# Scores of two slots in one stretch, softmax one slot ahead, in an attention and FFN kernel

## The reference

```python
def attention(query, key, value, mask, w_q, w_k, w_v, w_o):
    q = (query @ w_q).reshape(b, sq, 16, 64).transpose(0, 2, 1, 3)
    k = (key @ w_k).reshape(b, sk, 16, 64).transpose(0, 2, 1, 3)
    v = (value @ w_v).reshape(b, sk, 16, 64).transpose(0, 2, 1, 3)
    scores = einsum('bhqd,bhkd->bhqk', q, k) / sqrt(64)
    scores = where(mask, -inf, scores)
    out = einsum('bhqk,bhkd->bhqd', softmax(scores), v)
    return out.transpose(0, 2, 1, 3).reshape(b, sq, 1024) @ w_o

x = x + attention(layernorm(x), ctx, ctx, mask, w_q, w_k, w_v, w_o)
n = layernorm(x)
x = x + n @ int4_grid(kernel) + bias + (n @ lora_a) @ lora_b
```

## Time and profile before

| | |
|---|---|
| median of 3 runs | 492.87 us (491.85 to 492.99) |
| the profiled execution | 492.92 us, of which span 491.0 us |
| granted TensorE clock, mean | 0.987 |
| TensorE matmuls busy | 448.6 us, 91% of the span |
| VectorE busy | 405.4 us, 83% |
| GpSimd busy | 389.4 us, 79% |
| ScalarE busy | 329.7 us, 67% |
| DMA | 70.34 MB, mean 143 GB/s |

### The profile page before, as it was taken

One profiled execution on the slowest core, in us unless ns is written; L12 is line 12 of the kernel. 1 busy time (PEld: TensorE's weight loads), 2 busy tenths in 40 slices (PEclk: granted clock), 3 DMA queues, 4 the chain that ended last, 5 costly groups with the idle time before them and its releaser, 6 DMA issues.

```text
span 491.0 us, 15523 instructions
## 1 busy us (share of the span) xinstructions
PE 448.6 (91%) x5879; PEld 326.3 (66%) x5879; DVE 405.4 (83%) x1116; ACT 329.7 (67%) x851; POOL 389.4 (79%) x647
## 2 busy tenths in 40 slices
PE   3879989899999999999999999999999999989984
PEld 1435646786667866777666866777766866677772
DVE  4886689897988889787997979888988988888872
ACT  5968656866568766776677766776677766676631
POOL 5786777999788978789788988888787978688821
PEclk9889999999999999999999999999999999999997
DMA  8602996698767996789866995788877877659831
GB/s 290 215 23 46 140 205 107 119 207 172 148 124 145 191 142 119 123 185 160 144 130 126 189 179 119 136 175 171 134 127 138 144 157 143 130 97 171 136 85 37
DMA packets 212673, 70.34 MB, mean 143 GB/s; under 512 B 196641, under 2 KB 210738, under 8 KB 212594
## 3 DMA queue, kind: packets, MB, share of 16 engines
q1 hardware_dynamic: 211536, 67.68, 72.2%
q0 software_dynamic: 480, 1.31, 0.9%
q10 hardware_dynamic: 578, 0.30, 0.2%
HBM read 14.71 MB, written 4.19 MB: 39 GB/s over the span
## 4 chain that ended last, share of the span: by engine, by line
PE 42%; DVE 30%; ACT 18%; issue 4%; POOL 3%; DMA 2%; SPq 0%; DVEq 0%; POOLq 0%; ACTq 0%
PE ps_b L949 32%; ACT arena L704 9%; DVE ps_a L833 9%; PE ps_a L1017 6%; DVE arena L826 4%; DVE arena L899 3%; ACT arena L683 2%; DVE arena L815 2%; DVE arena L866 2%; DMA arena<-in_L_xattn_w_q_dram 2%; ACT arena L695 2%; DVE arena L837 2%; PE ps_b L1076 2%; ACT arena L650 2%; PE ps_b L1040 1%
## 5 line engine op out<-in xcount | busy, mean ns | idle before, releaser
L949 PE MATMUL ps_b<-arena 128*128 128x65 f16 (+3 forms) x3324 | 317.4, 247 | 8.2 <-DVE arena L899 5.1
L949 PEld LDWEIGHTS ps_b<-arena 128*128 128x128 f16 x3324 | 218.7, 98 | 83.1 <-issue 8.7
L704 ACT ACTIVATE arena<-ps_a,arena 128x160 f32<-128x160 f32 x512 | 159.6, 396 | 89.0 <-DVE arena L837 86.5
L613 POOL TENSOR_TENSOR arena<-arena 128x512 f16<-128x512 f32 x122 | 141.6, 1161 | 0.0
L608 POOL CAST arena<-arena 128x512 f16<-128x512 f32 x122 | 74.5, 611 | 54.5 <-ACT arena L704 53.1
L833 DVE TENSOR_REDUCE ps_a<-ps_a 128x4 f32<-128x640 f32 x128 | 105.3, 822 | 0.0
L1017 PE MATMUL ps_a<-arena 64*128 64x160 f16 x1536 | 75.4, 231 | 10.5 <-ACT arena L704 10.5
L1017 PEld LDWEIGHTS ps_a<-arena 64*128 64x128 f16 x1536 | 50.2, 94 | 35.3 <-issue 20.8
L1040 PE MATMUL ps_b<-arena 128*128 128x65 f16 x512 | 71.0, 193 | 0.0
L899 DVE TENSOR_TENSOR arena<-ps_b,arena 128x256 f32<-128x256 f32 x128 | 54.3, 424 | 4.4
L826 DVE TENSOR_TENSOR arena<-ps_b,arena 128x512 f16<-128x512 f32 x60 | 41.1, 686 | 19.9 <-ACT arena L695 18.7
(11 more groups left out here) (146 smaller groups left out, 436.6 us busy)
## 6 DMA issues: line engine op xcount, KB each, us to landing
arena<-in_x_dram SPq DMA_DIRECT2D x8, 512.0 KB, 5.5
mask_u<-in_x_dram SPq DMA_DIRECT2D x32, 128.0 KB, 3.0
out_dram<-mask_u SPq DMA_DIRECT2D x32, 128.0 KB, 2.7
arena<-arena SPq DMA_TRANSPOSE x128, 4.0
arena<-arena SPq DMA_DIRECT2D x24, 65.0 KB, 2.7
arena<-in_L_xattn_w_q_dram SPq DMA_DIRECT2D x1, 1024.0 KB, 8.5
arena<-in_L_xattn_w_k_dram SPq DMA_DIRECT2D x1, 1024.0 KB, 10.5
arena<-in_L_xattn_w_v_dram SPq DMA_DIRECT2D x1, 1024.0 KB, 12.3
```

Source lines behind the costliest of these rows:

```text
L613: nc.gpsimd.tensor_tensor(lo_main, main, hi_main, ALU.subtract)
L704: ins = nc.scalar.activation(probs[k % 2][:, h, :], p_scores[k % 2][:, h % 2, h // 2 * WINDOW:(h // 2 + 1) * WINDOW], ACT.Exp, bias=neg_ma ...
L949: mm = nc.tensor.matmul(dst, a, c, start=(first and at == 0), stop=(last and at == n - 1))
```

## The change

Five things are changed, and no arithmetic.

- TensorE makes scores(k+2) and scores(k+3) one after the other in even slots k, and none in odd ones.
- ScalarE makes exps(k+2) in slot k, in place of exps(k+1).
- VectorE makes maxima(k+2) in slot k: in odd slots behind the first projection, where maxima(k+1) stood, in even slots behind all projections and late items of slot k-1.
- GpSimd splits k+1 and SP transposes k+1 in slot k; there are five buffers for transposed probabilities in place of four, and the power of a tile's norm is made in the fourth slot of a tile in place of the third.
- The items p of the last batch are made one slot earlier.

```diff
-    PV_BEHIND, HALF_BUFS, TURN_BUFS = 3, 3, 4
+    PV_BEHIND, HALF_BUFS, TURN_BUFS = 3, 3, 5
...
-            if k in ON_PE:
-                late.append(("p", k))
+            if k + 1 in ON_PE:
+                late.append(("p", k + 1))
...
             def slot(s):
-                if s.k < LAST:
-                    turn_probs(s.k)
+                if s.k == 0:
+                    turn_probs(0)
+                if s.k + 1 < LAST:
+                    turn_probs(s.k + 1)
...
             def slot(s):
-                if s.k < LAST - 1:
-                    split_probs(s.k)
-                if s.k == LAST - 2:
-                    split_probs(LAST - 1)
+                if s.k == 0:
+                    split_probs(0)
+                if s.k + 1 < LAST:
+                    split_probs(s.k + 1)
                 tile = s.k // NG - 2
-                if s.g == 2 and 0 <= tile < NT:
+                if s.g == 3 and 0 <= tile < NT:
...
-                if DEEP - 1 <= s.k < LAST - 1:
-                    exps(s.k + 1)
+                if DEEP - 2 <= s.k < LAST - 2:
+                    exps(s.k + 2)
...
-                first = 1
+                even = s.k % 2 == 0
+                first = len(b.proj) if b and even else 1
                 if b:
                     for i, name in enumerate(b.proj[:first]):
                         item(b, i, name)
-                if DEEP - 1 <= s.k < LAST - 1:
-                    maxima(s.k + 1)
+                if DEEP - 2 <= s.k < LAST - 2 and not even:
+                    maxima(s.k + 2)
...
                         tail_item(b, len(b.proj) + i, name, tile)
+                if DEEP - 2 <= s.k < LAST - 2 and even:
+                    maxima(s.k + 2)
...
             def slot(s):
-                if DEEP - 2 <= s.k < LAST - 2:
+                if DEEP - 2 <= s.k < LAST - 2 and s.k % 2 == 0:
                     scores(s.k + 2)
+                    scores(s.k + 3)
                 if 0 <= s.k - PV_BEHIND < LAST:
                     weighted_values(s.k - PV_BEHIND)
```

More of the change, by code:

```diff
@@ L441, in probs_item @@
         def probs_item(k):
-            proj, late = slot_items(k)
-            return items_at[k] + len(proj) + late.index(("p", k)) + 1
+            proj, late = slot_items(k - 1)
+            return items_at[k - 1] + len(proj) + late.index(("p", k)) + 1
         def mains_split(k):
@@ L712, in norm_apply, with tail_item @@
                                      scale=ln_rstd[:, t:t + 1]).then_inc(xn_made, 1)
-            def tail_item(s, i, name):
+            def tail_item(s, i, name, tile):
                 act.wait_ge(item_made, s.item(i, 1))
@@ L717, in tail_item @@
                 if name == "p":
-                    ins = nc.scalar.activation(pT[s.k % TURN_BUFS][:, 0].rearrange("p h q -> p (h q)"), bank[:, :],
+                    ins = nc.scalar.activation(pT[tile % TURN_BUFS][:, 0].rearrange("p h q -> p (h q)"), bank[:, :],
                                                ACT.Copy)
@@ L756, in slot @@
                     item(s, i, name)
-                for i, (name, _) in enumerate(s.late):
+                for i, (name, tile) in enumerate(s.late):
                     if name in SPLIT:
-                        tail_item(s, len(s.proj) + i, name)
+                        tail_item(s, len(s.proj) + i, name, tile)
                 if s.norm_ahead and s.u >= NS - ST:
@@ L859, in tail_item @@
                 if name == "p":
-                    turn = pT[s.k % TURN_BUFS]
+                    turn = pT[tile % TURN_BUFS]
                     nc.vector.tensor_tensor(turn[:, 1].rearrange("p h q -> p (h q)"), bank[:, :],
@@ L1066, in tail_item @@
                 if name == "p":
-                    pe.wait_ge(exp_made, s.k + 1)
+                    pe.wait_ge(exp_made, tile + 1)
                     for e in range(GROUP):
-                        mm = nc.tensor.transpose(bank[:, e * P:(e + 1) * P], probs[s.k % 2][:, e, 0:P], ident[:, :])
+                        mm = nc.tensor.transpose(bank[:, e * P:(e + 1) * P], probs[tile % 2][:, e, 0:P], ident[:, :])
                 elif name[0] == "o":
```

## The result

The changed kernel takes 550.49 us in the median of 4 runs (547.14 to 552.05), and the kernel before 492.93 us beside it (491.85 to 494.77). The ratio is 1.1147, 95% interval 1.1115 to 1.1179: slower by 57 us. The profiled execution has a span of 550.2 us, 59.2 more than that of before.

What follows compares the result with a forecast made beforehand. TensorE bounds the kernel before; changed, a loop through VectorE and ScalarE would. Six batches at +5.5 us plus 3 for batch 0 and 0 for the last give +36 on 492.9: 529 us, range 512 to 544.

Steps and rivals of the forecast that it cites:

- The loop over VectorE and ScalarE: Batches 1 to 6: once a pair, 1.96 us from maxima over exponentials to high half lies nearly bare; 14.55 us a tile.
- pair B: From a tile's third slot to the next first, VectorE's way through its items, normalise and maxima: 7.45 us.
- pair A: From a tile's first slot to its third, VectorE's low halves, normalise, residual sum and maxima: 7.10 us.
- The bank: Three item banks: the output projection is ready at about 5.5, VectorE is there at 4.97; adds 0.5 us a tile.
- The rival without it: The output projection's bank doesn't bind, VectorE's loop alone sets the pace: +27 us, 520 us; chance 0.17.
- The sum over the middle: Batches 1 to 6: 60.8 us a batch against 55, taken as +5.5 us in each of six.
- the keys' discount: Keys make one tile some 0.3 us shorter, values one longer; only keys counted, so +5.8 a batch became +5.5.
- Batch 0: 1.3 us bare in each of 7 pairs is 9 us against 6 us of VectorE slack: +3 us (0 to 6).
- The last batch: No projections, so VectorE's odd-slot maxima follow at once and nothing is bare: 0 us (-2 to +2).
- Softmax a slot ahead: GpSimd's splits and SP's transposes for k+1 in slot k, five buffers; neither queue should be late: cost 0.
- The rivals above 540: More waits, 1 us a tile, 545 to 555 us; or TensorE's clock at 0.8 on the mean, 550 us; chance 0.12.
- The faster rival: TensorE stays the bound, saving 14 us and 5 us of waits for exponentials: 474 us; chance 0.06.

Runs made afterwards that it cites:

- The filler: Changed kernel plus 12 needless matmuls ahead of the weighted values in the second slot of each tile of the last batch; 543.73 us, ratio 1.1024.
- fifth experiment: Kernel before with only softmax, splits and transposes a slot ahead, fifth buffer, later power and earlier items p; scores singly, maxima early; 520.04 us, ratio 1.0556.
- third experiment: Kernel before with only the even slots' maxima of k+1 moved behind all projections and late items of k-1; 550.85 us, ratio 1.1135.
- first experiment: Changed kernel with maxima of k+2 behind the first projection in every slot, even ones too; pairs of scores stay; 514.16 us, ratio 1.0391.

## Why the prediction was wrong where it was

It said 529 us, at most 544; it came to 550. The sign held, and so did the mechanism in batches 1 to 6. By the profiled executions 59 us were lost in place of 36: of the 23 us missing, 10 are in the last batch, 8 in the middle and 5 in batch 0.

*The loop over VectorE and ScalarE: right, to a tenth.* Forecast for pair B 7.45 us, measured 7.46; for pair A with the bank and two statistics 7.10 + 0.51 + 0.15 = 7.76, measured 7.76. That this loop paces batches 1 to 6 whatever TensorE gains is shown from three sides: the late maxima alone give a batch of 61.2 us; 6.8 us of TensorE's work taken away leave it at 61.1 in the two batches in which the clock stayed up, and shorten none; and either way of opening the loop brings it to 56.4. One sign was misjudged: VectorE's waits for L697 came to 32.4 us and not to 50 to 70. It is all five lines of high halves of the projections together that wait 70.1 us (before 37.7).

*The bank: right.* Forecast 0.5 us a tile, measured 0.48 by taking the projection's length away. The pair of 7.76 us above doesn't test it, since 7.10 + 0.66 of statistics alone would give the same; in the other tiles of batch 4 L881 waits 0.48, 0.48 and 0.68 us for the projection. The rival without it is out.

*The sum over the middle: 8 us too small.* I forecast 6 x 5.5 = 33 us and it was 40.6. The base was no help: it was 331.7 us, not 330. The six batches took 372.3 us, where the forecast has 6 x 60.5 = 363. Of these 9.3 us, 3.0 are batch 2, which has the three items for the shared rests and took 64.1 us; 1.5 are one fall of the clock in batch 5, 62.6 us; 1.8 are the keys' discount; 1.8 are batches of 61.1 us where the sum without the discount gives 60.8. The last 1.2 us lie at the ends of the stretch. The discount was half of a pair of terms. The tile with the keys was 0.3 us under 15.06 as I said (14.78), but the one with the values 0.4 over it (15.44), and I had named both and counted one.

*Batch 0: 8.3 us in place of 3.* I counted bare waits against slack. I left out that the FFN work stands ahead of the late maxima in even slots and that TensorE waits for the normalise behind them, 3.09 us at 79.2. Behind that wait the output projection took 4.45 us in place of 2.78.

```profile
79.22 0.25 PE L954 MATMUL ps_b<-arena 128*128 128x65 f16 x3 [3.09 <-DVE arena L901]
79.70 4.45 PE L954 MATMUL ps_b<-arena 128*128 128x256 f16 x24
```

*The last batch: 10.2 us with the tail in place of 0.* This is the step that failed. "No projections, so that nothing is bare" looked at one ring only, VectorE's with ScalarE. Where it is open, another one closes through TensorE and the late maxima, here over the normalise that the weighted values wait for; I had listed that wait and never worked its ring through. The filler puts 1.7 of the 2.9 us a tile on the clock. The rest doesn't split into parts that add up. From slot 112 to the end it is 64.5 us before, 68.5 with softmax a slot ahead alone (fifth experiment), 74.5 with the late maxima alone (third) and 74.7 with both. A tile with early maxima and softmax ahead is 12.3 us, singly or in pairs, against 10.7 before.

*Softmax a slot ahead: costed at 0, costs 27 us alone.* The text looked at the queues that the step is moved past, GpSimd and SP, and found them free; they were. It didn't ask what VectorE's maxima then wait for: scores of the same slot. In the changed kernel this is hidden, since its loop is longer than the tie: a batch takes 54.8 us before, 57.4 with softmax ahead, 61.2 with late maxima and 61.1 with both, so the parts don't add up. That is why 27 and 57 make 57.

*The tile's power: misread, without effect.* It moved from the third slot of a tile to the fourth, where the text has it from the second to the third. ScalarE's activation that needs it waited for GpSimd twice in the run, 1.9 us in all, so that the cost of 0 held.

*The pairs: 14 us of work forecast, 6 us seen.* The shorter stretch is there: in the first experiment the matmul behind 24 scores starts 0.93 us after the first of them (464.37 to 465.30), against 2 x 0.52 before. The 6 us were gained over the tie of that experiment; on TensorE's bound alone the pairs weren't measured. The waits of scores for exponentials fell from 10.5 to 4.5 us, as said.

*The clock: underpriced.* I took the mean share, 81% busy at 1.00, as cover. In the changed kernel it fell behind single waits of 1.2 to 3.1 us, with the mean share at 84%. Which waits bring it down stays open. In the third experiment TensorE waits 1.73 us at the same place in five batches; the granted clock of the ten us around it was 0.83 in two of them and 1.00 in three.

*The rivals above 540* named the time, by luck: the clock was 0.964 to 0.976 on the mean and not 0.8, and the middle batches took 9 us more than forecast in 24 tiles, 0.4 us a tile and not 1. *The faster rival* (474 us, if the way round were under 1.4 us) is out by the measured 1.97 us. Even with the way round covered the kernel stays at 514. What stays open: no version here beats the kernel before, and whether the tie could be loosened with a third PSUM buffer for scores wasn't tried. That the tie itself costs the 27 us is read from the two waits and, in the last batch, from the sum of its ring; what was shown by a run is that softmax ahead with its buffer, the later power and the earlier items p costs it.

## What to carry to other kernels

When a step is moved in an engine's order, work out every ring of waits that closes through it, not only the one that shows first. Here they are maxima to exponentials to high half, and scores to maxima to normalise to weighted values. The longest ring is the floor: gains elsewhere don't lower it, and the next one stands right behind. A stage in which the first ring is open has to be worked out by the second. And if a consumer is moved a slot earlier while its producer stays, that gains no lead; it loses a slot of slack.

## What the runs showed of the hardware

Twelve needless matmuls in each of four slots (1.47 us a time in the trace) made the kernel 7 us faster: TensorE stayed at 2.4 GHz, where without them it fell to 1.2 GHz behind each of three waits of 1.42 and 1.43 us. Where it fell, 24 matmuls of 256 columns took 4.25 and 4.45 us against 2.78. The busy share doesn't tell where it falls: TensorE was busy for 6.84 us from 70 to 80 us of the changed kernel's run with the clock at 1.00, and for 8.07 us from 360 to 370 with 0.83. Nor does the length of one wait: behind 1.73 us it fell twice in five times in the third experiment.
